# Keys' norms by square root and reciprocal, and products and row products given to GpSimd, in a recurrent layer with routed experts

## What is computed

```python
q = silu(x @ Wq); k = l2_norm(silu(x @ Wk)) per head; v = x @ Wv
f = sigmoid(x @ Wf1 @ Wf2);  a = -k * sigmoid(x @ Wgamma) * f
for t in range(512):            # S: one 16 x 16 state per sequence and head
    S = S * f[t][:, None]
    S = S + k[t][:, None] * (a[t] @ S + v[t])[None, :]
    o[t] = q[t] @ S
s = layernorm(o * sigmoid(x @ Wog1 @ Wog2)) * norm_w @ Wo
```

## Time and profile before

| what | time |
|---|---|
| runs, median of 3 | 1158.05 us (1154.82 to 1160.11) |
| profiled execution | 1154.32 us |
| its span in the profile | 1152.6 us |
| mean granted clock of TensorE | 0.892 of full |

### The profile page before, as it was taken

One profiled execution on the slowest core, in us unless ns is written; L12 is line 12 of the kernel. 1 busy time (PEld: TensorE's weight loads), 2 busy tenths in 40 slices (PEclk: granted clock), 3 DMA queues, 4 the chain that ended last, 5 costly groups with the idle time before them and its releaser, 6 DMA issues.

```text
span 1152.6 us, 17274 instructions
## 1 busy us (share of the span) xinstructions
PE 905.7 (79%) x3893; PEld 707.7 (61%) x3893; DVE 1070.2 (93%) x3292; ACT 461.7 (40%) x1182; POOL 927.1 (80%) x921
## 2 busy tenths in 40 slices
PE   5999978215439999999999999989999872587771
PEld 2444434105328888878888887878888662476650
DVE  3899999999999999999999999999999999999995
ACT  5877767300003333333333233323233220787761
POOL 3888767357767888888898888888888888989883
PEclk9999989556659999999999999999999995988975
DMA  5656566665237676667776666756666515566322
GB/s 159 199 188 220 166 225 204 215 199 154 94 106 192 209 215 199 199 175 212 215 214 208 186 198 210 215 176 199 190 200 200 172 40 150 158 169 174 97 72 64
DMA packets 238292, 202.76 MB, mean 176 GB/s; under 512 B 140528, under 2 KB 216272, under 8 KB 238224
## 3 DMA queue, kind: packets, MB, share of 16 engines
q1 hardware_dynamic: 161184, 82.93, 26.9%
q10 hardware_dynamic: 70224, 100.49, 26.5%
q0 software_dynamic: 6816, 18.69, 4.6%
HBM read 139.54 MB, written 62.54 MB: 175 GB/s over the span
## 4 chain that ended last, share of the span: by engine, by line
POOL 45%; DVE 29%; issue 17%; SPq 3%; DMA 3%; PE 1%; ACT 1%; POOLq 0%; DVEq 0%; ACTq 0%
POOL prod_q L385 16%; POOL prod_a L368 14%; POOL y_d L603 5%; DVE obh L1319 3%; DVE ubuf L1335 3%; DVE prod_a L1328 2%; SPq L393 2%; DMA rec_d<-work 2%; DVE state L1360 1%; POOL rbh L660 1%; POOL obh L347 1%; DVE prod_a L1353 1%; POOL cross L657 1%; POOL rbh L663 1%; DVE outer L1345 1%
## 5 line engine op out<-in xcount | busy, mean ns | idle before, releaser
L368 POOL TENSOR_TENSOR prod_a<-state,rbh 128x512 f32<-128x512 f32 x203 | 258.2, 1272 | 83.1 <-DVE state L1393 72.8
L1010 PE MATMUL psA<-xT,wts 128*128 128x256 f32 x1248 | 288.1, 387 | 23.8 <-ACT work L804 23.1
L1010 PEld LDWEIGHTS psA<-xT,wts 128*128 128x128 f32 x1248 | 239.5, 194 | 66.2 <-ACT work L804 32.1
L1021 PE MATMUL psF<-wts,work 128*128 128x256 f32 x1248 | 277.3, 381 | 0.0
L1021 PEld LDWEIGHTS psF<-wts,work 128*128 128x128 f32 x1248 | 235.3, 191 | 30.7
L385 POOL TENSOR_TENSOR prod_q<-state,rbh 128x512 f32<-128x512 f32 x178 | 226.1, 1270 | 0.0
L804 ACT ACTIVATE work<-psA,b_sb 128x256 f32<-128x256 f32 x312 | 129.3, 472 | 189.0 <-PE psA L1010 148.8
L1319 DVE TENSOR_REDUCE obh<-prod_q 128x16 f32<-128x272 f32 x480 | 204.0, 426 | 0.0
L815 ACT ACTIVATE work<-psF,work 128x256 f32<-128x256 f32 x78 | 37.0, 474 | 198.7 <-PE psF L1021 198.7
L1382 DVE TENSOR_REDUCE ubuf<-prod_a 128x16 f32<-128x272 f32 x203 | 87.2, 429 | 27.3 <-POOL prod_a L368 27.3
L546 POOL TENSOR_TENSOR rinv<-ssm,neghalf 128x16 f32<-128x16 f32 x32 | 98.6, 3080 | 2.7
(11 more groups left out here) (195 smaller groups left out, 1566.8 us busy)
## 6 DMA issues: line engine op xcount, KB each, us to landing
wts<-in_L_ffn_W_dram ACTq DMA_DIRECT2D x78, 1024.0 KB, 5.4
rec_d<-work SPq DMA_DIRECT2D x32, 768.0 KB
rbh<-rec_d SPq DMA_DIRECT2D x32, 768.0 KB, 5.7
xs_d<-zero SPq DMA_DIRECT2D x26, 387.0 KB, 10.8
work<-xs_d ACTq DMA_DIRECT2D x39, 258.0 KB, 5.6
wts<-y_d ACTq DMA_DIRECT2D x16, 512.0 KB, 5.9
x_acc<-in_L_attn_x_dram SPq DMA_DIRECT2D x32, 128.0 KB
o_d<-obh SPq DMA_DIRECT2D x32, 128.0 KB, 6.7
```

The lines of the kernel that those rows point to most:

```text
L368: eng.tensor_tensor(prod_a[:, n, 1:3, :, 0:HD], state[:, g % SR, :, :].unsqueeze(1).broadcast_to(wide), rows.unsqueeze(2).broadcast_to(wid ...
L1010: mm = pe.matmul(psA[m // 2 % 2][:, m % 2 * MT:(m % 2 + 1) * MT], w1_sb[v][:, c, m * P:(m + 1) * P], xgT[:, c, :], start=(c == 0), stop=(c ...
L1021: mm = pe.matmul(psF[q][:, 0:D], hT[:, m, q * P:(q + 1) * P], w2_sb[v][:, m, :], start=(m == 0), stop=(m == FC - 1))
```

## The change

ACT takes the square root of the sums of squares (`roots`, Sqrt, one instruction for a group of two tiles, behind both `sigmoids`), and DVE takes the reciprocal (`invert`); the clamp becomes the min of `scale_k`. POOL's `factors` keeps only the product of f and gamma. For pairs 1 to 27 (READS) POOL makes the states' products for the outputs (`read_rows_of`) in place of DVE's `read_left` and `read_found`. For chunks 1 to 6 POOL makes the row products: those of chunks 1 to 3 between the tiles, of chunk 4 after the last tile, of chunks 5 and 6 between the scatter's DMAs. The ring `rec` has 7 tiles, the rings of f2 and gamma 4. `scale_k` and `scale_a` in pair g now serve tile g + 2, so the last tile's fall into pair 29. The diff, cut (the new `prepare_part` is the old one, moved, with one more wait; semaphores' names and mere index changes are left out):

```diff
@@ -31,7 +31,7 @@
...
-RS = 5
+RS = 7
@@ -48,6 +48,7 @@
...
+READS = range(1, 28)
@@ -112,13 +113,15 @@
...
-        rec = work[:, 0:RS * H * REC].rearrange("p (u h c) -> p u h c", u=RS, h=H)
-        f2 = wts[:, 0:2 * D].rearrange("p (u n) -> p u n", u=2)
-        ksq = wts[:, 2 * D:4 * D].rearrange("p (u n) -> p u n", u=2)
+        o1 = 6 * D
+        rec = [(wts[:, u * H * REC:(u + 1) * H * REC] if u < 5 else work[:, o1 + (u - 5) * H * REC:o1 + (u - 4) * H * REC])
+               .rearrange("p (h c) -> p h c", h=H) for u in range(RS)]
+        f2 = work[:, 0:4 * D].rearrange("p (u n) -> p u n", u=4)
+        ksq = work[:, 4 * D:6 * D].rearrange("p (u n) -> p u n", u=2)
@@ -316,7 +319,15 @@
         def prepared(c):
-            return 8 * min(c + 1, SHARED + 1) + (c >= SHARED - 1) + (c >= SHARED) + 3 * max(0, c - SHARED)
+            return sum(8 + (k > 0) if by_dve(k) else 2 + (k >= SHARED - 1) for k in range(c + 1))
+        def by_dve(c):
+            return c in (0, SHARED)
+        def parts(c):
+            return 3 * (c - 1 - (c > SHARED))
         def shared(g):
@@ -537,28 +548,66 @@
...
-            def factors(n, u, first, last):
-                pool.wait_ge(s_ss, n + 1)
-                pool.tensor_scalar(ssm[:, u, :], ss[:, u, :], 1e-24, None, ALU.max).then_inc(s_ssm, 1)
-                pool.wait_ge(s_ssm, n + 1)
-                if not first:
-                    pool.wait_ge(s_kn, n - 1)
-                pool.tensor_tensor(rinv[:, u, :], ssm[:, u, :], neghalf[:, 0:H], ALU.pow).then_inc(s_ng, 1)
+            def factors(n):
+                u = n % 4
...
+            def read_rows_of(g):
+                pool.wait_ge(s_chain, g * CHAIN + 1)
+                if g >= SR:
+                    pool.wait_ge(s_o, summed(2 * (g - SR)))
+                if g % NP == 0:
+                    pool.wait_ge(s_prep, prepared(g // NP))
+                    pool.wait_ge(s_pp, parts(g // NP) + 3)
+                    read_left(pool, g)
+                    read_found(pool, g)
+                else:
+                    if g == 1:
+                        pool.wait_ge(s_prep, prepared(0))
+                    read_both(pool, g)
+            def prepare_part(c, part):
+                u, done = c % RB, parts(c)
+                rows = rbh[:, u, :, :].rearrange("p (n j) c -> p n (j c)", j=2)
+                wide = [P, NP, 2, HD]
+                def both(column):
+                    return rows[:, :, column:column + HD].unsqueeze(2).broadcast_to(wide)
+                qa = rows[:, :, Q_:2 * REC - Q_].rearrange("p n (s w) -> p n s w", s=2)[:, :, :, 0:HD]
+                fk = rows[:, :, F_:2 * K_ - F_].rearrange("p n (s w) -> p n s w", s=2)[:, :, :, 0:HD]
+                if part == 0:
+                    pool.wait_ge(s_prep, prepared(c - 1))
+                    pool.wait_ge(s_rb[u], c // RB * 16 + 16)
+                    pool.tensor_tensor(cross.rearrange("p s n k -> p n s k"), qa, both(K_), ALU.mult).then_inc(s_pp, 1)
+                if part == 1:
+                    pool.wait_ge(s_pp, done + 1)
+                    pool.tensor_tensor(qa, qa, both(F_), ALU.mult).then_inc(s_pp, 1)
+                if part == 2:
+                    pool.wait_ge(s_pp, done + 2)
+                    pool.tensor_tensor(fk, fk, both(REC + F_), ALU.mult).then_inc(s_pp, 1)
...
             for n in range(3):
-                factors(n, n % 2, n < 2, False)
+                factors(n)
...
-            for n in range(3, NT):
-                factors(n, n % 2, False, False)
-                if n == NT // 4:
+            factors(3)
+            for g in range(NT - HEAD):
+                if g in READS:
+                    read_rows_of(g)
+                factors(g + HEAD)
+                c, part = divmod(g - 4, NP)
+                if part < 3 and 0 <= c < 3:
+                    prepare_part(c + 1, part)
+                if g == NP:
...
+            for part in range(3):
+                prepare_part(4, part)
@@ -578,12 +627,16 @@
...
                 scatter(n, 0)
+                if n in (12, 14, 16):
+                    prepare_part(5, (n - 12) // 2)
...
                 scatter(n, 1)
+                if n in (4, 6, 8):
+                    prepare_part(6, (n - 4) // 2)
             def number(t):
@@ -761,6 +803,7 @@
...
                     sigmoids(n)
+                roots(group[0], group[-1])
@@ -731,26 +764,35 @@
...
             def sigmoids(n):
-                u, u4 = n % 2, n % RS
+                u, v, u4 = n % 2, n % 4, n % RS
...
-                if n >= 2:
-                    act.wait_ge(s_rec, n - 1)
-                act.activation(gam[:, u, :], psB[u][:, D:D + H], ACT.Sigmoid).then_inc(s_gam, 1)
...
+                if n >= 4:
+                    act.wait_ge(s_rec, n - 3)
+                act.activation(gam[:, v, :], psB[u][:, D:D + H], ACT.Sigmoid).then_inc(s_gam, 1)
...
+            def roots(first, last):
+                act.wait_ge(s_ss, last + 1)
+                if first >= 2:
+                    act.wait_ge(s_ng, last - 1)
+                if first == last:
+                    act.activation(root[:, first % 2, :], ss[:, first % 2, :], ACT.Sqrt).then_inc(s_rt, 1)
+                else:
+                    act.activation(root[:, :, :], ss[:, :, :], ACT.Sqrt).then_inc(s_rt, 2)
@@ -1153,21 +1196,29 @@
...
-                    dve.wait_ge(s_ssm, n - 1)
+                    dve.wait_ge(s_rt, n - 1)
...
+            def invert(n):
+                u = n % 2
+                dve.wait_ge(s_rt, n + 1)
+                if n >= 2:
+                    dve.wait_ge(s_kn, n - 1)
+                dve.reciprocal(rinv[:, u, :], root[:, u, :]).then_inc(s_ng, 1)
             def scale_k(n):
...
-                dve.tensor_tensor(rec[:, u4, :, K_:K_ + HD], rec[:, u4, :, K_:K_ + HD],
-                                  rinv[:, u, :].unsqueeze(2).broadcast_to([P, H, HD]), ALU.mult).then_inc(s_kn, 1)
+                dve.scalar_tensor_tensor(out=rec[u4][:, :, K_:K_ + HD], in0=rinv[:, u, :].unsqueeze(2).broadcast_to([P, H, HD]),
+                                         scalar=1e12, in1=rec[u4][:, :, K_:K_ + HD], op0=ALU.min, op1=ALU.mult).then_inc(s_kn, 1)
             def scale_a(n):
-                u, u4 = n % 2, n % RS
+                v, u4 = n % 4, n % RS
...
-                dve.scalar_tensor_tensor(out=rec[:, u4, :, A_:A_ + HD], in0=rec[:, u4, :, K_:K_ + HD], scalar=-1.0,
-                                         in1=heads(f2[:, u, :]), op0=ALU.mult, op1=ALU.mult).then_inc(s_rec, 1)
+                dve.scalar_tensor_tensor(out=rec[u4][:, :, A_:A_ + HD], in0=rec[u4][:, :, K_:K_ + HD], scalar=-1.0,
+                                         in1=heads(f2[:, v, :]), op0=ALU.mult, op1=ALU.mult).then_inc(s_rec, 1)
             def route():
@@ -1290,16 +1341,17 @@
...
-                if c >= SHARED - 1:
+                if c > 0:
...
             def prepared_rows(c, u):
-                dve.wait_ge(s_pp, 3 * (c - SHARED))
+                dve.wait_ge(s_pp, parts(c) + 3)
...
-                dve.tensor_copy(home_a, tok[:, :, 0, A_:A_ + HD]).then_inc(s_prep, 1)
+                if c >= SHARED - 1:
+                    dve.tensor_copy(home_a, tok[:, :, 0, A_:A_ + HD]).then_inc(s_prep, 1)
@@ -1333,7 +1385,10 @@
...
-                if g > 0:
+                if g == READS.stop:
+                    dve.wait_ge(s_q, 2 * g - 1)
+                if g > 0 and g not in READS:
@@ -1345,17 +1400,18 @@
...
                 if tile is not None:
+                    invert(tile - 2)
...
-                    scale_k(tile - 1)
+                    scale_k(tile - 2)
...
-                if g - 2 not in range(*SUMS):
+                if g - 2 not in range(*SUMS) and g not in READS:
...
                 if tile is not None:
-                    scale_a(tile - 1)
+                    scale_a(tile - 2)
@@ -1401,7 +1457,7 @@
...
-                if c <= SHARED:
+                if by_dve(c):
@@ -1423,19 +1479,24 @@
...
-                        two_steps(c * NP + n, slots + n if slots is not None and slots + n <= NT else None)
+                        two_steps(c * NP + n, slots + n if slots is not None and slots + n <= NT + 1 else None)
...
-            for n in range(HEAD):
-                square_sums(n)
-                if 0 < n < len(STATS) - 2:
-                    in_stats(n + 2)
-                if n + 1 < HEAD:
-                    scale_k(n)
-                    scale_a(n)
-                if n == 0:
-                    in_stats(n + 2)
+            def scaled(n):
+                invert(n)
+                scale_k(n)
+                scale_a(n)
+            square_sums(0)
+            scaled(0)
+            in_stats(2)
+            square_sums(1)
+            in_stats(3)
+            square_sums(2)
+            in_stats(4)
+            scaled(1)
+            square_sums(3)
```

(35 more changed lines are left out.)

8 lines of the change are left out of this document (2 added, 6 removed).

## The result

The changed kernel takes 1176.71 us (median of 4 runs, 1176.06 to 1179.64), the kernel before 1156.77 beside it (4 runs): a ratio of 1.0162, 95% interval 1.0141 to 1.0183. The profiled execution's span is 1175.2 us against 1152.6.

The account below looks back on a forecast made before the run. VectorE was taken as full in the stage of tiles, with ScalarE looped with PE. Terms: +5.3 stage, +6.2 later scatter, +6.5 row products, -4.3 POOL's former idle, sum +13.7, on 1158.05 giving 1172 us; range 1155 to 1190.

Parts of the forecast that it names:

- VectorE's pair in the stage: Pairs 0 to 27: 5.2 us without interference plus 0.8 for POOL's product, 6.0 us per pair on VectorE.
- the stage term: Pairs 0 to 27: 6.1 us a pair plus 0.7 for each of three chunk boundaries, 172.9 against 167.6, +5.3 us.
- The price of one product: Stage of tiles: POOL's state product delays VectorE by 0.3 to 0.93 us a pair, taken 0.8, with POOL mostly waiting.
- the sign that was named: Stage of tiles: behind each new state stands POOL's product, and L1328's successor lasts about 1.6 us instead of 0.67.
- Row products in "POOL's free time": Stage of tiles: the row products, 0.73 us each, go into POOL's free time and add nothing.
- The root's load: ScalarE, stage of tiles: one more table load of 1.28 us per group of two tiles, bringing a group to 11.67 us.
- The product ahead of the scatter: Behind pair 28: last record and zeros go out after the routing, so the scatter starts 4.5 to 8.0 us later, taken +6.2.
- Six row products between the scatters: POOL's scatter: six row products lengthen it by 4.4 to 10.4 us, taken +6.5.
- Faster, since Sqrt needs no load: Rival: Sqrt needs no load of its own, VectorE alone decides, port price 0.15, pair 5.35 us; 1151 us, chance 12%.
- Within 0.5%: Rival: products fall into one-operand sums, PE's clock holds, ScalarE's 5.83 us a pair decides; 1160 to 1164 us, chance 18%.
- The clock rival: Rival: PE's holes lower the clock in every group, 6.6 us per pair, +27.7, 1186 us; chance 15%.
- The small rival that POOL's powers had held VectorE: Rival: the powers on POOL do hold VectorE in the stage, so their removal gives time back; 1%, within the 12%.

Follow-up runs that it names:

- e2: Changed kernel with a sigmoid in place of the square root, so no table load for the root: 1171.1 us, ratio 1.0107 to the kernel before.
- e10: Changed kernel with all products back on VectorE, a sigmoid for the root (no load), last tile scaled ahead of the routing: 1157.4 us, ratio 0.9995.
- e12: e10 with the states' products of pairs 1 to 27 on POOL again: 1163.8 us, ratio 1.0055 to the kernel before.
- e1: Changed kernel with the states' products of pairs 1 to 27 back on VectorE; row products stay on POOL: 1171.9 us, ratio 1.0112.
- e8: Changed kernel with states' products and row products of chunks 1 to 6 back on VectorE, the root's load kept: 1170.4 us, ratio 1.0118.
- e11: Changed kernel with states' products back on VectorE, a sigmoid for the root (no load), last tile scaled ahead of the routing: 1162.7 us, ratio 1.0042.
- e9: Changed kernel with the row products of chunks 1 to 6 back on VectorE: 1175.5 us, ratio 1.0157 to the kernel before.
- e4: Changed kernel with only the row products of chunks 5 and 6 back on VectorE: 1175.3 us, ratio 1.0134 to the kernel before.
- e3: Changed kernel with the last tile's reciprocal and two scalings moved ahead of the routing: 1172.2 us, ratio 1.0114 to the kernel before.
- e6: Changed kernel with the states' products back on VectorE and a sigmoid for the root (no load): 1164.6 us, ratio 1.0062.
- c1: Kernel before, with zeros issued four tiles earlier and GpSimd's shared pairs begun at pair 50 instead of 53: 1156.4 us, ratio 0.9989.
- r1: Kernel before, with only the row products of chunks 1 to 6 moved to GpSimd: 1161.4 us, ratio 1.0037.

## Why the prediction was right, and what was mis-sized

- **The sum.** Predicted +13.7 us on the span, measured +22.6: +1.1 from a later pair 0, +13.0 in the stage (predicted +5.3), +8.5 behind it (predicted +8.4). The forecast's direction held in both places, slower in the stage and in the tail. Its size held only in the tail, and there by luck, as shown below; the stage grew by more than twice what was forecast. That the total came out near is helped by the baseline: by the medians the change is +19.9.
- **The step that was mis-sized is VectorE's pair in the stage, above all the row products in it, which were put at nothing.** The prediction had 28 x 6.0 + 2.1 = 170.1 us for VectorE by itself, and 6.1 per pair with ScalarE's loop beside it. e2, where VectorE has no idle time, shows 176.6; of the 7.7 us that the stage term lacked, 6.5 are this. Of e2's 35.6 us of lengthening, 7.8 stand already in e10, where POOL makes none of the products that were moved (6.9 before the change). The prediction has them inside its 5.2 per pair, for the pair with a quiet POOL takes 4.97. Another 21.0 are the states' products (e12 against e10), put at 28 x 0.8 = 22.4. The 6.8 that are left (e2 against e12) are the row products'. With one execution for each stage, this split is good to 2 to 3 us.
- **The price of one product was right, its reason and its place wrong.** e12 against e10 has 0.78 us per pair (taken: 0.8), e1 against the changed kernel 19.1 / 27 = 0.71. But POOL does not stand waiting for the state: in the stage it waits 92.8 us for gamma and once, 4.8 us, for the state. The products come late and in pairs, and fall on whatever VectorE does then. So the sign that was named, L1328's successor at about 1.6 us, did not come: L1380 lasts 0.87 in the mean, and L1383 and L1400 pay as well.
- **Row products in "POOL's free time"** were put at nothing in the stage. e1 has 5.7 us more lengthening than e8 for nine of them, 0.6 each, against 3.2 us less own work, and the run with them is 5.3 longer (e11 against e10): POOL's time was free, VectorE's was not. In the changed kernel itself this price is not seen: e9, without its row products, has 0.6 us less lengthening, and its run is not shown to differ. Pairs 29 to 52 became 2.0 us longer, where the prediction had them 3.9 shorter for VectorE. About 1.0 of this is the last tile's three instructions, which make pair 29 last 5.51 us instead of 4.55; and from the start of pair 29 to that of pair 52 e4, with the row products of chunks 5 and 6 on VectorE, takes 1.9 less than the changed kernel (103.2 against 105.2).
- **The root's load.** One per group and 1.28 us, as predicted, with nothing behind it (75.13 to 76.41, the root at 76.42). The Trainium skill, "ScalarE: Activation LUTs", section "What ACT_TABLE_LOAD costs", adds a drain of about 1.38 us to each load; this load shows none either. The load's share of the stage was 172.9 - 170.1 = 2.8 in the sum and 4.0 in e2. Taking the later of two loops as the pace was too simple: VectorE and ScalarE wait for each other by turns, 7.2 and 8.8 us, and a group takes 13.14 us, where VectorE alone needs 12.6 (e2) and the prediction had 11.67 for ScalarE alone.
- **The clock** was 0.88 of full speed in the stage against 0.90; e2, without the load, shows 0.89 in a stage 4 us shorter. No run here separates its share.
- **The tail.** The product ahead of the scatter, against pair 28: 261.45 - 225.21 instead of 238.71 - 211.10, +8.6 (taken 6.2, bounds 4.5 to 8.0; the first scatter itself +8.2). Six row products between the scatters: the scatter is 4.9 longer (taken 6.5). POOL's former idle: 4.6 (taken 4.3). Three errors that cancel, so that the tail came out right is luck. DVE's wait in pair 53 was 4.71 and not about 10, since pair 28 and pairs 29 to 52 took 3.2 us more and made VectorE late as well; e3 agrees that the tail by itself was worth only that wait.
- **The rivals.** "Faster, since Sqrt needs no load" had its condition made true in e2 and e12, and they were still slower (1.0107, 1.0055): that rival's port price of 0.15 was what could not be had. "Within 0.5%" needed the products in the one-operand sums, and that they would be cheap there no run has tried. The clock rival needed a group of 13.2 us; the groups did take 13.14 us (load to load, mean of 13), but VectorE alone needs 12.6 us for the two pairs of a group (e2), so the clock does not have to explain them. The small rival that POOL's powers had held VectorE is out as well: without them the lengthening is 7.8 us in e10, and it was 6.9 before.

By parts, built up from e10: products on POOL +6.4 us (e12); row products +5.3, with the products back on VectorE (e11); the load +4.0 to 9.6 us of stage, the less the more POOL already holds VectorE; the late last tile 4.5 (e3). These prices are not a sum: the row products cost nothing that is shown beside the states' products and the load (e9), and the late tile nothing that is shown without them (e11). None of the parts was a gain.

## What to carry to other kernels

Moving work from a full VectorE to an idle GpSimd saved nothing here, where both read their operands from SBUF: before counting the saving, find in the trace how long a VectorE instruction lasts beside the GpSimd one, for every instruction that is moved, row products too. An engine with idle time is not free of cost in a loop: one table load per turn on ScalarE, busy for 80% of this stage, cost VectorE its waits. And a scatter that ended 12 us earlier (e3) was worth only the wait that ended on it.

## What the runs showed of the hardware that was not expected

- Both sides pay: POOL's 128x512 product, 1.27 us elsewhere, lasted 1.71 and 1.53 us beside VectorE's two-operand instructions, and 1.375 in the mean of e12's stage, while VectorE's 0.42 became 1.49.
- The same 14 table loads cost 4.0, 6.1 and 9.6 us of stage (changed kernel against e2, e1 against e6, e8 against e10). In these three the load costs less the longer VectorE is busy without it: own work and lengthening are 176.1 us in e2, 170.7 in e6 and 167.8 in e10.
- ScalarE's waits for spills in the stage (work rows and table rows together) are 20.5 us in the one trace of the kernel before, 34.7 in c1, 37.4 in r1, and none in any kernel with the ring of seven. c1 sent zeros earlier and r1 did not, and each was profiled once, so neither the zeros nor the row products are shown to lengthen these waits.
